# Cross-attention with image tokens: one wait split in the output product, one K load cut in two, one output weight loaded a step later

## The chip, the cores and the metric

The kernel runs on one core of a Trainium2 chip. The metric is the device time of one execution in microseconds (us). Before the change three runs gave 409.63, 410.31 and 410.38 us; their median is 410.31 us.

## The reference

The layer is a cross-attention of 4096 query rows (2 batches of 2048) with 640 features and 20 heads of 32. Each batch has 77 context tokens: 69 of text and 8 for the image (4 dummy tokens, 4 for boxes), each group with weights and a softmax of its own.

```python
q = split_heads(x @ w_q)                       # 20 heads of 32
k = split_heads(text @ w_k);    v = split_heads(text @ w_v)        # 69 tokens, depth 1024
out_text = softmax(q @ k.T / sqrt(32)) @ v
k_ip = split_heads(ip @ w_k_ip); v_ip = split_heads(ip @ w_v_ip)   # 8 tokens
out_ip = softmax(q @ k_ip.T / sqrt(32) + mask_ip(bbox)) @ v_ip     # mask 0 or -10000
return (out_text + out_ip) @ w_out + b_out + x
```

Everything is float32. The kernel makes the products with w_q and w_out from high and low parts of their factors.

## The kernel before

**Units.** The work is 40 units, numbered c. A unit is one block of 128 of the 640 features (4 heads), g = c mod 5, for one tile of 512 query rows. Five units in a row, g = 0 to 4, are a group: one tile of rows of one batch. The features lie on the partitions, the rows on the free axis.

**Split products.** A factor such as x is stored as x_hi, its rounding to the matmul's reduced float format, and x_lo, the rest. A product over depth 640 is then 15 matmuls (`product`, L631 to L636): for each of five blocks kt of 128 of the depth, hi by hi, hi by lo and lo by hi, so that matmul n belongs to block n // 3. `make_q` makes the queries of a unit so, `make_out` its block of the output. The output of unit c needs the attention output of all five units of its group as its five depth blocks: matmuls 0 to 11 read the blocks of units c to c+3 of the group's first unit c, matmuls 12 to 14 the block of unit c+4.

**A unit's way.** TensorE makes the scores (`make_scores`, L666); VectorE takes the maximum and subtracts it (L499 to L516); ScalarE takes the exponential (L393); VectorE sums and inverts (L523 to L528); GpSimd multiplies by the inverse (L355, L357); VectorE transposes 32 by 32 blocks (L535); SyncE issues eight DMAs of the result (L257) and ScalarE four (L401); TensorE makes the attention output o (`make_o`, L680); ScalarE copies it to o_hi (L436); VectorE makes o_lo = o - o_hi (L541); later TensorE makes the output product, and VectorE adds bias and residual (`finish`, L553).

**Order of the work.** Every engine has an order of its own, written out by hand: a prologue, 40 steps, an epilogue. In step c of the middle part TensorE does `make_scores(c+1)`, `make_o(c-2)`, `make_q(c+2)`, `make_out(c-6)`. VectorE does the maximum and shift of unit c+1, `o_low(c-2)`, the transpose of c, the sums of c+1, `finish(c-6)`. ScalarE does `o_high(c-2)`, the exponential of c+1, the copy of q of c+2, its four DMA issues for c, and then the high parts of what was loaded in this step. GpSimd does the multiplication of c and then the low parts of what was loaded in step c-1. Each engine works its list strictly in order, so a wait holds everything behind it on that engine. `make_out(c)` with g = 0 waits until `o_low` of unit c+4 is done, which VectorE does in the same step; the last group's outputs are made by another function (`make_last`) in the epilogue.

**Loads.** x tiles and the five blocks of w_q and of w_out pass through five slots of a tile named stage, in the order of the list JOBS; SyncE loads a slot (L239), ScalarE makes the high part (L380 for x, L383 for weights), the low part follows on GpSimd (L339, L343). x of the next group is loaded in steps with g = 0 (three tiles) and g = 1 (two). WO_JOBS says in which steps the blocks of w_out are loaded: blocks 0 and 1 in step 4, 2 in step 6, 3 in step 7, 4 in step 8. The first output product is that of step 6.

**Prologue.** SyncE issues, in this order, w_q block 0, five tiles of x, the context, the first image K weights (wki), the first K weights (wk, 512 KB, L244), the grid, the boxes, the identity (eye), w_q 1, wk 1, wki 1, w_q 2; the next load waits for a K block to be finished. TensorE warms up, makes q of unit 0, then `k_image(0)` (L716), `k_text(0)` (L710, eight depth blocks), `k_fold(0)` (L734) and the scores of unit 0, then `k_text(1)` and more. In steps 0 to 5 it also makes the rest of K and V; for V block g the order is `v_image(g)` (L716), four matmuls of a q, `v_fold(g)` (L749), which waits until ScalarE has copied the image part (`copy_v_part`, L412), the rest of q with `v_turn(g)` (L754) in it.

Of the kernel before, what the change touches and what calls it, by code (L numbers as in the profile page):

```python
# [11 lines left out]
P = 128  # L12
# [13 lines left out]
KD = D // P  # L26
KC = C // P
# [12 lines left out]
K_SLOTS, V_SLOTS, AHEAD_K = 2, 3, 2  # L40
# [1 line left out]
V_OLD = {3: 0, 4: 2}  # L42
V_OLD_STEP = {V_OLD[g] + 1: g for g in V_OLD}
X_JOBS = {0: (0, 1, 2), 1: (3, 4)}
WO_JOBS = {4: (0, 1), 6: (2,), 7: (3,), 8: (4,)}
BEHIND_OUT = KD + 1


def xattn_kernel(nc, x, ctx, bbox, grid, eye, w_q, w_k, w_v, w_k_ip, w_v_ip, w_out, b_out, out):
# [5 lines left out]
    def sb(name, shape, dt=F32):  # L55

        at[name] = top[0]
        n = 4
        for s in shape[1:]:
            n *= s  # L60
        top[0] += -(-n // 32) * 32
        assert top[0] <= nc.sbuf_usable_end, (name, top[0], nc.sbuf_usable_end)
        return nc.alloc_sbuf_tensor_at(name, shape, dt, offset=at[name])

    def over(name, owner, shape, offset=0):

        return nc.alloc_sbuf_tensor_at(name, shape, F32, offset=at[owner] + offset)

    def sem(name):
        return es.enter_context(nc.semaphore(name))  # L70

    with es:
# [7 lines left out]
        k = sb("k", [P, BATCH, KD, TOKENS])  # L80
# [24 lines left out]
        half = KD * W * 4  # L105
        x0_raw = over("x0_raw", "o_lo", [P, KD, W])
        wk_raw = over("wk_raw", "o_hi", [P, K_SLOTS, KC, P], half)
# [29 lines left out]
        bias_loaded = sem("bias_loaded")  # L137
        ctx_loaded = sem("ctx_loaded")
        wk_loaded = [sem(f"wk_loaded{s}") for s in range(K_SLOTS)]
        wki_loaded = [sem(f"wki_loaded{s}") for s in range(K_SLOTS)]  # L140
        wv_loaded = [sem(f"wv_loaded{s}") for s in range(V_SLOTS)]
        wvi_loaded = [sem(f"wvi_loaded{s}") for s in range(V_SLOTS)]
# [27 lines left out]
        o_lo_done = sem("o_lo_done")  # L170
# [6 lines left out]
        def place(c):  # L177

            return (c // KD) % BATCH, c // (BATCH * KD), c % KD
# [23 lines left out]
        def out_bank(c):  # L203

            return Q_BANK if c == UNITS - BEHIND_OUT - 1 else OUT_BANK
# [10 lines left out]
        def step_jobs(c):  # L216

            if c in WO_JOBS:
                jobs = [("w_out", g) for g in WO_JOBS[c]]
            else:  # L220
# [10 lines left out]
        def _(sp):  # L231
            def load(job):

                what, n = job
                src, width = {"w_q": (w_q, D), "w_out": (w_out, D), "x": (x, W)}[what]
                number = NUMBER[job]
                if number >= KD:
                    sp.wait_ge(stage_lo, number - KD + 1)
                sp.dma_start(stage[:, number % KD, 0:width], src[n]).then_inc(stage_loaded[number % KD], 16)  # L239

            def load_k(g, dst, src, loaded):
                if g >= K_SLOTS:
                    sp.wait_ge(kt_made, g - K_SLOTS + 1)
                sp.dma_start(dst[:, g % K_SLOTS, :, :], src[g]).then_inc(loaded[g % K_SLOTS], 16)  # L244

            def load_v(g, dst, src, loaded):
                if g in V_OLD:
                    sp.wait_ge(vt_made, V_OLD[g] + 1)
                sp.dma_start(dst[:, V_SLOT[g], :, :], src[g]).then_inc(loaded[V_SLOT[g]], 16)
# [24 lines left out]
            def prologue():  # L274
                load(("w_q", 0))
                for kt in range(KD):
                    sp.dma_start(x0_raw[:, kt, :], x[kt]).then_inc(x0_loaded[kt], 16)  # L277
                sp.dma_start(ctx_sb[:, :, :], ctx).then_inc(ctx_loaded, 16)
                load_k(0, wki_raw, w_k_ip, wki_loaded)
                load_k(0, wk_raw, w_k, wk_loaded)  # L280
                sp.dma_start(grid_sb[:, :], grid).then_inc(grid_loaded, 16)
                sp.dma_start(box[:, :, :, :], bbox).then_inc(grid_loaded, 16)
                sp.dma_start(eye_sb[:, :], eye).then_inc(eye_loaded, 16)
                load(("w_q", 1))
                load_k(1, wk_raw, w_k, wk_loaded)
                load_k(1, wki_raw, w_k_ip, wki_loaded)
                load(("w_q", 2))
                load_k(2, wk_raw, w_k, wk_loaded)
                load_k(2, wki_raw, w_k_ip, wki_loaded)
                load(("w_q", 3))  # L290
                load_v(0, wv_raw, w_v, wv_loaded)
                load_v(0, wvi_raw, w_v_ip, wvi_loaded)
                load(("w_q", 4))
                load_v(1, wv_raw, w_v, wv_loaded)
                load_v(1, wvi_raw, w_v_ip, wvi_loaded)
                load_k(3, wk_raw, w_k, wk_loaded)
                load_k(3, wki_raw, w_k_ip, wki_loaded)
# [20 lines left out]
            def epilogue():  # L318
# [6 lines left out]
                for k in range(2):  # L325
                    sp.wait_ge(stored[k], 16 * (UNITS // 2))

            turns(prologue, step, epilogue)

        @block.gpsimd  # L330
# [297 lines left out]
        def _(pe):  # L628
            whole = range(3 * KD)

            def product(bank, w_hi, w_lo, m_hi, m_lo, b, g, n):  # L631

                kt = n // 3
                w, m = ((w_hi, m_hi), (w_hi, m_lo), (w_lo, m_hi))[n % 3]
                return nc.tensor.matmul(ps[:, bank, :], w[:, g, P * kt:P * kt + P], m[:, b, kt, :],  # L635
                                        start=(n == 0), stop=(n == 3 * KD - 1))  # L636
# [48 lines left out]
            def make_out(c):  # L685
                b, t, g = place(c)
                if g == 0:
                    pe.wait_ge(o_lo_done, c + KD)
                if c < KD:
                    pe.wait_ge(stage_lo, NUMBER[("w_out", g)] + 1)  # L690
                if out_bank(c) == Q_BANK:
                    pe.wait_ge(q_copied, UNITS)
                elif c >= 1:
                    pe.wait_ge(finished, c if out_bank(c - 1) == OUT_BANK else c - 1)
                for n in whole:
                    last = product(out_bank(c), wo_hi, wo_lo, o_hi, o_lo, b, g, n)
                last.then_inc(out_made, 1)

# [19 lines left out]
                last.then_inc(made, 1)  # L718

            def k_text(g, kts=range(KC)):  # L720
                pe.wait_ge(wk_loaded[g % K_SLOTS], 16 * (g // K_SLOTS + 1))
                if g >= 2:
                    pe.wait_ge(k_copied, g if g > 2 else 1)
                text_part(k_places[g], wk_raw[:, g % K_SLOTS, :, :], kts)
# [32 lines left out]
            def prologue():  # L757
                pe.wait_ge(zeros_set, 1)
                for n in range(WARM):
                    nc.tensor.matmul(ps[:, WARM_BANK, 0:P], q[:, 0, 0:P], q[:, 0, 0:P], start=True, stop=True)  # L760
                make_q(0, whole)
                pe.wait_ge(ctx_loaded, 16)
                k_image(0)
                k_text(0)
                k_fold(0)
                make_scores(0)
                k_text(1)
                make_q(1, whole[0:6])
                k_image(1)
                make_q(1, whole[6:15])  # L770
                k_text(2)
                k_fold(1)
                k_image(2)
# [103 lines left out]
```

## Time and profile before

| | |
|---|---|
| median of three runs | 410.31 us |
| profiled execution, its time | 409.03 us |
| profiled execution, its span | 407.2 us |
| TensorE busy with matmuls | 397.4 us, 98% |
| VectorE busy | 337.1 us, 83% |
| GpSimd busy | 155.9 us, 38% |
| ScalarE busy | 129.3 us, 32% |
| granted TensorE clock, mean | 1.000 |
| HBM read, written | 35.53 MB, 10.49 MB |

The span runs from the first to the last instruction; the time has the work around it as well, here 1.8 us. Matmuls are pipelined: a 128x512 matmul lasts some 0.39 us in the profile but the next one starts 0.23 us after it, so that the time of TensorE is read from the starts and not from the busy share. An idle time is shown in brackets with what ended it.

### The profile page before, as it was taken

The page shows a single profiled execution, that of the slowest core. Times are in us where ns is not written, and L with a number is a line of the kernel's source. Part 1 is how long each engine was busy: PE and PEld are TensorE (multiplying, and loading weights), DVE is VectorE, ACT ScalarE, POOL GpSimd, SP SyncE. Part 2 cuts the span into 40 slices and gives each one's busy share as a digit, 9 for nine tenths or more (in the row PEclk, how much of TensorE's full clock was granted, in tenths as well). Part 3 has the DMA queues.
Part 4 walks back from the last instruction along what each step waited for, and adds up shares of the span by engine and source line. Part 5 has one row for each costly group of instructions (what it writes and reads, how often), then busy time and mean ns, then how long its engine had stood idle before and what let it go on. Part 6 is the DMA issues. An engine that isn't in the chain of part 4 may idle for free.

```text
span 407.2 us, 10795 instructions
## 1 busy us (share of the span) xinstructions
PE 397.4 (98%) x4452; PEld 290.7 (71%) x4452; DVE 337.1 (83%) x458; ACT 129.3 (32%) x196; POOL 155.9 (38%) x128
## 2 busy tenths in 40 slices
PE   7899999899999999999999999999999999999996
PEld 6688878567777776777777767777776767776764
DVE  4559779899999988999989988999988898989523
ACT  5236343463333322432323322333223322232100
POOL 0336622686326433363226533462226532222200
PEclk9999999999999999999999999999999999999999
DMA  7999746675567455764566454764466453544655
GB/s 276 360 381 341 203 133 184 181 198 164 172 172 200 140 138 144 201 166 129 148 180 213 131 137 134 206 167 125 139 192 208 137 134 119 143 136 118 168 154 196
DMA packets 42849, 72.96 MB, mean 179 GB/s; under 512 B 10544, under 2 KB 10672, under 8 KB 42800
## 3 DMA queue, kind: packets, MB, share of 16 engines
q1 hardware_dynamic: 37680, 67.02, 54.3%
q10 hardware_dynamic: 5120, 5.25, 5.9%
q8 instruction: 35, 0.57, 0.6%
q14 instruction: 14, 0.11, 0.1%
HBM read 35.53 MB, written 10.49 MB: 113 GB/s over the span
## 4 chain that ended last, share of the span: by engine, by line
PE 81%; DVE 5%; DMA 5%; SPq 4%; issue 2%; ACT 2%; ACTq 1%; DVEq 0%
PE ps L635 59%; PE ps L666 8%; PE ps L680 8%; PE ps L710 3%; SPq L257 2%; DMA out_tiles<-res 2%; DMA wk_raw<-in_w_k 2%; DVE text_max L499 1%; DVE prob L505 1%; ACT prob L393 1%; ACTq L401 1%; PE ps L716 1%; DMA res<-in_x 1%; SPq L277 1%; SPq L268 1%
## 5 line engine op out<-in xcount | busy, mean ns | idle before, releaser
L355 POOL TENSOR_TENSOR prob<-prob,rden 128x1104 f32<-128x1104 f32 x40 | 82.3, 2056 | 205.5 <-DVE rden L528 205.5
L635 PE MATMUL ps<-x_hi,wq_hi 128*128 128x512 f32 x200 | 83.2, 416 | 1.6 <-DVE x_lo L597 1.6
L635 PE MATMUL ps<-o_hi,wo_hi 128*128 128x512 f32 x200 | 80.2, 401 | 0.4 <-DVE o_lo L541 0.4
L635 PE MATMUL ps<-o_hi,wo_lo 128*128 128x512 f32 x200 | 78.9, 395 | 0.0
L635 PE MATMUL ps<-o_lo,wo_hi 128*128 128x512 f32 x200 | 78.9, 395 | 0.0
L635 PE MATMUL ps<-x_lo,wq_hi 128*128 128x512 f32 x200 | 78.7, 394 | 0.0
L635 PE MATMUL ps<-x_hi,wq_lo 128*128 128x512 f32 x200 | 78.1, 391 | 0.0
L393 ACT ACTIVATE prob<-prob 128x1232 f32<-128x1232 f32 x40 | 50.0, 1250 | 68.9 <-DVE prob L516 68.9
L535 DVE STREAM_TRANSPOSE prob_t<-prob 128x1536 f32<-128x1536 f32 x40 | 70.6, 1766 | 0.2 <-POOL prob L357 0.2
L499 DVE TENSOR_REDUCE text_max<-ps 128x16 f32<-128x1104 f32 x40 | 52.1, 1303 | 19.5 <-PE ps L666 19.4
L635 PEld LDWEIGHTS ps<-x_hi,wq_hi 128*128 128x128 f32 x200 | 37.5, 187 | 36.8 <-issue 28.0
L523 DVE TENSOR_REDUCE den<-prob 128x16 f32<-128x1104 f32 x40 | 50.5, 1263 | 7.1 <-ACT prob L393 7.1
L436 ACT ACTIVATE o_hi<-ps 128x512 fp32r<-128x512 f32 x40 | 23.7, 593 | 102.8 <-PE ps L680 98.9
L505 DVE TENSOR_TENSOR prob<-ps,text_max 128x1104 f32<-128x1104 f32 x40 | 51.9, 1299 | 0.0
L635 PEld LDWEIGHTS ps<-o_hi,wo_hi 128*128 128x128 f32 x200 | 37.5, 188 | 14.8 <-issue 3.4
L553 DVE SCALAR_TENSOR_TENSOR res<-ps,bias,res 128x512 f32<-128x512 f32 x37 | 27.4, 741 | 22.3 <-PE ps L635 11.2
L339 POOL TENSOR_TENSOR x_lo<-stage,x_hi 128x512 fp32r<-128x512 f32 x35 | 44.8, 1305 | 2.7 <-ACT x_hi L380 2.7
L635 PEld LDWEIGHTS ps<-o_hi,wo_lo 128*128 128x128 f32 x200 | 37.5, 188 | 9.3
L635 PEld LDWEIGHTS ps<-o_lo,wo_hi 128*128 128x128 f32 x200 | 37.5, 188 | 8.5
L635 PEld LDWEIGHTS ps<-x_hi,wq_lo 128*128 128x128 f32 x200 | 37.6, 188 | 8.2
L666 PEld LDWEIGHTS ps<-k,q 32*64 32x64 f32 x2560 | 32.6, 130 | 14.4 <-issue 12.6
L680 PE MATMUL ps<-prob_k,v 77*32 77x512 f32 x320 | 42.6, 605 | 0.3 <-DMA prob_k<-prob_t 0.3
(58 smaller groups left out, 350.1 us busy)
## 6 DMA issues: line engine op xcount, KB each, us to landing
prob_k<-prob_t SPq DMA_DIRECT2D x320, 64.0 KB
stage<-in_x SPq DMA_DIRECT2D x38, 256.0 KB, 3.1
res<-in_x SPq DMA_DIRECT2D x37, 256.0 KB
out_tiles<-res SPq DMA_DIRECT2D x37, 256.0 KB, 2.3
prob_k<-prob_t ACTq DMA_DIRECT2D x160, 32.0 KB
wki_raw<-in_w_k_ip SPq DMA_DIRECT2D x5, 512.0 KB, 7.4
wk_raw<-in_w_k SPq DMA_DIRECT2D x5, 512.0 KB, 7.3
wv_raw<-in_w_v SPq DMA_DIRECT2D x5, 512.0 KB, 7.3
```

Of the source, the lines that this page charges most:

```text
L339: nc.gpsimd.tensor_tensor(x_lo[:, b, kt, :], slot[:, 0:W], x_hi[:, b, kt, :].bitcast(F32), ALU.subtract).then_inc(stage_lo, 1)
L355: nc.gpsimd.tensor_tensor(e[:, :, 0:TEXT], e[:, :, 0:TEXT], rden[:, par, 0, :].unsqueeze(2).to_broadcast([P, QT * HG, TEXT]), ALU.mult)
L393: nc.scalar.activation(prob[:, c % 2, :, 0:TOKENS], prob[:, c % 2, :, 0:TOKENS], ACT.Exp).then_inc(exp_done, 1)
L436: nc.scalar.activation(o_hi[:, b, g, :], ps[:, O_BANK, :], ACT.Copy).then_inc(o_hi_done, 1)
L499: nc.vector.tensor_reduce(text_max[:, par, :, :], s[:, :, :, 0:TEXT], AX_X, ALU.max).then_inc(text_max_done, 1)
L505: nc.vector.tensor_tensor(e[:, :, :, 0:TEXT], s[:, :, :, 0:TEXT], text_max[:, par, :, :].unsqueeze(3).to_broadcast([P, QT, HG, TEXT]), ALU ...
L523: nc.vector.tensor_reduce(den[:, par, 0, :], e[:, :, 0:TEXT], AX_X, ALU.add)
L535: nc.vector.transpose(prob_t[:, c % 2, :, :, :].rearrange("p k n r -> p n k r"), prob[:, c % 2, :, :].rearrange("p n (k r) -> p n k r", r= ...
L553: nc.vector.scalar_tensor_tensor(out=tile, in0=ps[:, bank, :], scalar=bias[:, c % KD:c % KD + 1], in1=tile, op0=ALU.add, op1=ALU.add).then ...
L635: return nc.tensor.matmul(ps[:, bank, :], w[:, g, P * kt:P * kt + P], m[:, b, kt, :], start=(n == 0), stop=(n == 3 * KD - 1))
L666: last = nc.tensor.matmul(ps[at:at + P // 2, j, TOKENS * n:TOKENS * n + TOKENS], q[rows, c % 2, P * n + at:P * n + at + P // 2], k[rows, b ...
L680: last = nc.tensor.matmul(ps[DH * j:DH * j + DH, O_BANK, :], v[0:TOKENS, b, P * g + DH * j:P * g + DH * j + DH], p_k[:, :, :, j, :], start ...
```

## The change

Three things are changed. First, `make_out` of a group's first unit waits at its start for four `o_low` of the group's five and for the fifth before its matmul 12, the thirteenth. Second, the first K weights are loaded by two DMAs of four depth blocks each, with a semaphore each, and `k_text(0)` is called in two halves that wait for one semaphore each; the counts of the other K loads are shifted to match. Third, block 1 of w_out is loaded in step 5, behind the three x tiles of that step, where it was loaded in step 4; its high part moves on ScalarE from step 4 to step 5, its low part on GpSimd from step 5 to step 6.

```diff
-WO_JOBS = {4: (0, 1), 6: (2,), 7: (3,), 8: (4,)}
+WO_JOBS = {4: (0,), 5: (1,), 6: (2,), 7: (3,), 8: (4,)}
...
+        wk0_loaded = [sem(f"wk0_loaded{h}") for h in range(2)]
...
-                load_k(0, wk_raw, w_k, wk_loaded)
+                for half in range(2):
+                    kts = slice(KC // 2 * half, KC // 2 * half + KC // 2)
+                    sp.dma_start(wk_raw[:, 0, kts, :], w_k[0].rearrange("p (k n) -> p k n", n=P)[:, kts, :]).then_inc(wk0_loaded[half], 16)
...
                 if g == 0:
-                    pe.wait_ge(o_lo_done, c + KD)
+                    pe.wait_ge(o_lo_done, c + KD - 1)
...
                 for n in whole:
+                    if g == 0 and n == 3 * KD - 3:
+                        pe.wait_ge(o_lo_done, c + KD)
                     last = product(out_bank(c), wo_hi, wo_lo, o_hi, o_lo, b, g, n)
...
             def k_text(g, kts=range(KC)):
-                pe.wait_ge(wk_loaded[g % K_SLOTS], 16 * (g // K_SLOTS + 1))
+                if g == 0:
+                    pe.wait_ge(wk0_loaded[kts[0] * 2 // KC], 16)
+                else:
+                    pe.wait_ge(wk_loaded[g % K_SLOTS], 16 * ((g + 1) // K_SLOTS))
...
-                k_text(0)
+                k_text(0, range(0, KC // 2))
+                k_text(0, range(KC // 2, KC))
```

## Rows read from the trace of the kernel before

**Rows 1.** Busy time by stretch: length, busy (instructions) by engine, clock, DMA share, GB/s.

```profile
100.00:363.00 263.00, 262.94 (x2959) 188.69 (x2958) 237.46 (x320) 81.25 (x114) 105.12 (x85) 1.00 0.56 158
```

**Rows 2.** Waits, whole span: us in total, times, longest.

```profile
PEld ps L635 <- DVE o_lo L541: 3.1, 7, 0.8
```

**Rows 3.** Timeline of PE at three of the seven first output products: start, us.

```profile
83.96 0.39 PE L635 MATMUL ps<-x_hi,wq_lo 128*128 128x512 f32 x1
...
85.05 0.39 PE L635 MATMUL ps<-o_lo,wo_hi 128*128 128x512 f32 x1
...
129.70 0.39 PE L635 MATMUL ps<-x_hi,wq_lo 128*128 128x512 f32 x1
...
130.44 0.39 PE L635 MATMUL ps<-o_lo,wo_hi 128*128 128x512 f32 x1
...
356.82 0.39 PE L635 MATMUL ps<-x_hi,wq_lo 128*128 128x512 f32 x1
...
357.29 0.39 PE L635 MATMUL ps<-o_lo,wo_hi 128*128 128x512 f32 x1
```

**Rows 4.** Timeline of DVE and PE in the first q product, which waits five times.

```profile
7.14 2.66 DVE L597 TENSOR_TENSOR x_lo<-x_raw,x_hi 128x512 fp32r<-128x512 f32 x4 [1.18 <-ACT x_hi L442]
...
9.86 0.39 PE L635 MATMUL ps<-x_hi,wq_lo 128*128 128x512 f32 x1
10.09 0.39 PE L635 MATMUL ps<-x_hi,wq_hi 128*128 128x512 f32 x1
```

**Rows 5.** Timeline of PE, first K block and start of the second.

```profile
11.57 0.64 PE L716 MATMUL ps<-wki_raw,ctx_sb 128*32 128x128 f32 x16 [0.63 <-DMA wki_raw<-in_w_k_ip]
12.84 2.15 PE L710 MATMUL ps<-ctx_sb,wk_raw 128*128 128x138 f32 x16 [0.62 <-DMA wk_raw<-in_w_k]
...
16.46 2.15 PE L710 MATMUL ps<-ctx_sb,wk_raw 128*128 128x138 f32 x16
```

**Rows 6.** Timeline of SP's queue, the five x tiles.

```profile
1.18 2.32 SPq L277 DMA_DIRECT2D x_raw<-in_x  x5
```

**Rows 7.** DMA issues of x tiles four and five: KB, us to landing.

```profile
x_raw<-in_x SPq DMA_DIRECT2D x1, 256.0 KB, 5.2
...
x_raw<-in_x SPq DMA_DIRECT2D x1, 256.0 KB, 5.3
```

**Rows 8.** DMA issues at 6.05 (eye) and 7.28 (second K block): us to landing.

```profile
eye_sb<-in_eye SPq DMA_DIRECT2D x1, 72.0 KB, 7.3
...
wk_raw<-in_w_k SPq DMA_DIRECT2D x1, 512.0 KB, 7.9
```

**Rows 9.** Timeline of ACT and PE in step 5, at v_fold(4).

```profile
73.21 1.37 ACT L383 ACTIVATE wo_hi<-stage 128x640 fp32r<-128x640 f32 x2 [3.56 <-issue]
74.48 0.26 ACT L412 ACTIVATE img_part<-ps 128x128 f32<-128x128 f32 x1
...
73.94 0.40 PE L635 MATMUL ps<-x_hi,wq_hi 128*128 128x512 f32 x1
74.79 0.40 PE L749 MATMUL ps<-eye_sb,img_part 128*128 128x16 f32 x2 [0.46 <-ACT img_part L412]
```

**Rows 10.** Timeline of DVE, ACT and POOL in step 6 and at its end.

```profile
83.97 0.68 DVE L541 TENSOR_TENSOR o_lo<-ps,o_hi 128x512 fp32r<-128x512 f32 x1
...
88.50 0.75 DVE L553 SCALAR_TENSOR_TENSOR res<-ps,bias,res 128x512 f32<-128x512 f32 x1 [0.40 <-PE ps L635]
...
81.36 1.68 ACT L380 ACTIVATE x_hi<-stage 128x512 fp32r<-128x512 f32 x3 [2.66 <-issue]
82.94 0.58 ACT L436 ACTIVATE o_hi<-ps 128x512 fp32r<-128x512 f32 x1
...
82.60 3.86 POOL L339 TENSOR_TENSOR x_lo<-stage,x_hi 128x512 fp32r<-128x512 f32 x3
```

**Rows 11.** Landing times of all loads into the stage slots.

```profile
DMA to landing us min/median/max: 2.2/3.1/8.9
```

**Rows 12.** Timeline of DVE at the scores of the last unit.

```profile
370.94 1.31 DVE L499 TENSOR_REDUCE text_max<-ps 128x16 f32<-128x1104 f32 x1 [0.45 <-PE ps L666]
```

## The prediction

> **What bounds the kernel now.** Read the page first: TensorE is busy 98% of the span, VectorE 83%, the rest far less, the clock is at full throughout. The table of stretches sharpens this: between 100 and 363 us, 29 steps, TensorE has 262.94 of 263.00 us and VectorE 237.46 [rows 1]. VectorE so has 25.5 us to spare, 0.88 us in each step. The reader is to see that in this stretch only time on TensorE counts, and that a gain there is followed by VectorE as long as it is under 0.88 us a step. But busy is no proof of full pace, as ends of matmuls are modelled. So I read the waits next: the weight load ahead of the output product waits for o_lo seven times, 3.1 us in all [rows 2], which the matmul row hides. Last the timeline, start by start, at each of these seven places and wherever TensorE's row shows a bracket. Those in the part that the diff touches: 0.62 us for the first K weights [rows 5] and 0.46 us for the copied image part of V block 4 [rows 9].
>
> **The late wait in make_out.** What one wait costs is the distance from the last q matmul to the second output matmul. Where nothing is late it is 357.29 - 356.82 = 0.47 us, two normal steps [rows 3]. In the first output product it is 85.05 - 83.96 = 1.09, so 0.62 us are lost; at 129.70 it is 0.74, so 0.27. The four like it, at 175, 220, 266 and 311 us, read 0.71, 0.73, 0.73 and 0.77: 0.24, 0.26, 0.26 and 0.30. The seventh, at 356.82, loses nothing. Sum: 0.62 + 0.27 + 0.24 + 0.26 + 0.26 + 0.30 + 0 = 1.95 us. (The 3.1 us of rows 2 count the idle weight load, which in a full stream also rests between loads, so the starts are the better measure.)
>
> After the change the product starts behind the q product, and the wait comes twelve matmuls later, at 0.233 us each 2.8 us. o_lo was late by at most 0.7 us. So it is there 2 us ahead, and what is late next is nothing on this path. Twelve of the fifteen matmuls are issued before the wait; queued behind it are the last three and then the next scores, which VectorE waits for, but only if the wait bites.
>
> Does a satisfied wait amid a product cost anything? The first q product has such waits, at its matmuls 3, 6, 9 and 12. x_lo of the fifth tile is done by 7.14 + 2.66 = 9.80 us; the thirteenth matmul starts at 10.09, 0.23 us behind the one before it [rows 4]. That is the normal distance: the price is nil, here with no more than 0.3 us in hand. I take 0 for seven added waits and 1.95 us gained. For the bounds: were each satisfied wait to cost a quarter of a matmul step, 0.06 us, it would be 0.4 us in seven.
>
> Does the gain stay? VectorE waits for TensorE both at finish (0.40 us, at 88.50) [rows 10] and at the next maximum (0.45 us, as at 370.94) [rows 12]; each group of five steps gets 0.27 us shorter against five times 0.88 us to spare. At 370.94 VectorE still waits for the last scores, so that what follows, the transpose, its DMAs and the chain of stores and residual loads which ends the kernel, starts earlier by as much as TensorE does. This chain of some 30 us is of waits between DMAs, none bound to a fixed time; I price its change at 0, with 0.5 us of chance either way.
>
> **First K weights in halves.** k_image(0) starts at 11.57, as its weights land; its sixteen short matmuls hold until 12.21. k_text(0) starts at 12.84, as wk has landed [rows 5]. The two 512 KB transfers land 1.27 us apart, so half of one takes some 0.64 us: the first half lands at about 12.1, before TensorE is free, the second at 12.8. Four of the eight depth blocks take about 1.0 us (all eight take 2.15 us, less a modelled tail of some 0.2), so the second half is called at 13.2 and has 0.4 us in hand. Gain: 12.84 - 12.24 = 0.60 us.
>
> Smaller transfers might be slower, with rows of 2 KB where they were 4 KB. The x tiles have such rows: tile five is issued 0.47 us after tile four [rows 6] and takes 5.3 where that took 5.2 us [rows 7], so they land 0.57 us apart, 256 KB each; at the pace of the K weights 256 KB take 0.64. No loss, then. One more issue costs SyncE 0.47 us [rows 6] for everything behind it in the prologue; these transfers take 7.3 to 8.3 us to land where the same kind takes 3.1 later [rows 8, 11], so they stand in line and an issue 0.5 us later changes nothing. Were it to, by the whole 0.47: the identity lands at 6.05 + 7.3 + 0.47 = 13.8, before the fold that wants it (about 14.2); wk 1 lands at 7.28 + 7.9 = 15.2, or 15.7, and is wanted at 16.46 - 0.60 = 15.86. Behind that the loads wait for the fold of block 0 and so move with it. I keep 0.60, with 0.2 to 0.65 as bounds.
>
> The Trainium skill speaks against this edit: "DMA: Bandwidth & Descriptors", in its section on the anatomy of one DMA, gives each DMA a constant part of about 2.0 us beside its bytes, and its section on bandwidth wants transfers of 1 MiB and up. If the two halves paid that one after the other, by its figures the second half would land some 2 us later, an estimate from that page. Rows 7 show the opposite for transfers in line, 0.57 us apart, and so the rule, which measures one alone, gets a small chance below.
>
> **w_out block 1 a step later.** In step 5 ScalarE makes two high parts, from 73.21 to 74.58, and only then copies the image part of V block 4, at 74.48; TensorE stops after the matmul of 73.94 and starts v_fold(4) at 74.79 [rows 9]. Unheld it would start at 73.94 + 0.23 = 74.17: 0.62 us lost. With one high part fewer (half of the 1.37, some 0.65 us) the copy starts at 73.83 and is done at 74.09 + a little: v_fold(4) starts on time. Gain 0.62 us, at worst 0.5. SyncE's issue of that load (0.46 us) moves behind the x loads of step 5, ahead of a residual that is wanted twelve us later.
>
> What it adds in step 6: on ScalarE, in front of the copy to o_hi of unit 4 at 82.94 [rows 10], 0.65 us. The copy then ends near 83.59 + 0.58 = 84.2 and o_lo of unit 4 starts at 84.2 for 83.97 and ends at 84.9. Before the change this would have been on TensorE's path; now the thirteenth matmul waits for it, and that one is due at 83.96 + 0.23 - 0.62 + 2.80 = 86.4. It has 1.5 us in hand. VectorE itself runs 0.25 us later and has the 0.40 and the 0.45 us. On GpSimd the low part (about 1.3 x 640/512 = 1.6 us) runs behind the three x tiles, 82.60 + 3.86 + 1.6 = 88.1, as the sums of unit 7 are ready (88.50 - 0.40): no delay, at worst 0.1. The block itself is wanted by the second output product at 93 us.
>
> **Sum.** 1.95 + 0.60 + 0.62 = 3.17 us. The profiled execution took 409.03 us (span 407.2), which gives 405.9 (span 404.0). It was 1.28 us faster than the median of the three runs, so against that median: 410.31 - 3.2 = 407.1 us.
>
> **The rivals.**
> - One small term fails: a load behind the split, or the stop at v_fold, stays. The 0.4 us in hand for the second half and the exact fit at 74.17 speak for it. Gain 3.2 - 0.6 = 2.6 us: 407.7.
> - Transfers pay their fixed part each (the page's rule, told with rows): the shortest landing of a stage load is 2.2 us [rows 11]. If the second half took that behind the first, 12.1 + 2.2 = 14.3, k_text(0) would end at 15.3 for 14.8: 0.5 us lost instead of 0.6 gained. Gain 2.1: 408.2. The tiles of x speak against it.
> - The tail absorbs it: the last 30 us hang on SyncE's stores and residual loads, and if these start no earlier the end stays. 410.3. Against it: VectorE's 0.45 us wait at 370.94.
> - Slower: the moved load. It stands behind three x loads, issued at about 76.4 us by SyncE's timeline, and ScalarE, strictly in order, wants it at 83.0. Should it land later, o_lo of unit 4 and TensorE at the thirteenth matmul are late by as much beyond 1.5 us. With the longest landing of any stage load, 8.9 us [rows 11], it comes at 85.3 and costs 85.3 - 83.0 - 1.5 = 0.8 us: still faster. It turns the sign only from a landing 83.0 + 1.5 + 3.2 + 0.8 = 88.5 on, 12 us after its issue, as four times the median of 3.1 us; then 411.2.
>
> **How the numbers follow.** Forecast 0.70, one term failing 0.14, fixed parts 0.05, tail 0.06, slower 0.03; 0.02 remain for the unthought. About 0.2%, 0.8 us, is what a measurement of this kernel can tell from no change. So faster 0.90, same 0.07, slower 0.03. The runs before span 0.75 us; with the bounds of the terms (gain 2.4 to 3.8) and that, the range is 406.0 to 408.7 us, which holds the first two rivals as well.
>
> **What would show it.** In the trace after: no wait of PE or PEld for o_lo, and 0.23 us between all starts at the six places; k_text(0) at 12.2 to 12.3 without a stop at its fifth block; v_fold(4) 0.23 us behind its matmul; o_lo of unit 4 about 0.2 us later against the scores of its step; the clock still 1.00. I am wrong if a wait of 0.3 us or more turns up at a thirteenth matmul, if K loads behind the split hold TensorE, if the scores or make_o begin to wait in the middle part, or if the last 30 us grow.

## The result, and the profile after

The changed kernel took 406.56 us (median of six runs, 405.89 to 407.92) beside 409.51 us for the kernel before on the same chip (six runs, 409.27 to 410.38). The medians are 2.95 us apart; the ratio on record is 0.9917, with an interval of 0.9900 to 0.9933: 3.4 us faster, 2.7 to 4.1. The forecast was 407.1 us and a gain of 3.2, counted from a median of three runs of 410.31 us; the six runs' median is 0.8 us lower. One run of all those told below was slow (414.56 us, the kernel with the moved load alone), and the ratios leave it out. The profiled execution took 406.34 us with a span of 404.5, so 2.7 us less than the profiled execution before.

The page of the changed kernel, its span and its busy time by engine:

```profile
span 404.5 us, 10796 instructions
...
PE 396.8 (98%) x4452; PEld 292.2 (72%) x4452; DVE 337.2 (83%) x458; ACT 129.5 (32%) x196; POOL 155.8 (39%) x128
```

Its stretch of 100 to 363 us, same columns as [rows 1]:

```profile
100.00:363.00 263.00, 263.00 (x2964) 190.24 (x2963) 238.33 (x322) 82.78 (x114) 103.76 (x84) 1.00 0.57 160
```

The busy share hardly moved (TensorE 262.94 to 263.00 us of 263.00); five more matmuls went through the same 263 us. That is all a busy row can show of a gain of 1.2 us here. The list of waits of the changed kernel has no row in which TensorE or its weight load waits for o_lo, where [rows 2] had 3.1 us. The starts show where the gain is. The timeline of TensorE after, at the places of [rows 5], [rows 9] and [rows 3], and at the last attention output (L638 is the former L635, L715 L710, L721 L716, L757 L749, L669 L666):

```profile
11.33 0.64 PE L721 MATMUL ps<-wki_raw,ctx_sb 128*32 128x128 f32 x16 [0.60 <-DMA wki_raw<-in_w_k_ip]
11.90 2.15 PE L715 MATMUL ps<-ctx_sb,wk_raw 128*128 128x138 f32 x16
...
73.31 0.40 PE L638 MATMUL ps<-x_hi,wq_hi 128*128 128x512 f32 x1
73.55 0.39 PE L757 MATMUL ps<-eye_sb,img_part 128*128 128x16 f32 x2
...
77.51 0.95 PE L669 MATMUL ps<-k,q 32*64 32x77 f32 x64 [0.69 <-ACT q L392]
...
82.69 0.39 PE L638 MATMUL ps<-x_hi,wq_lo 128*128 128x512 f32 x1
83.15 0.39 PE L638 MATMUL ps<-o_lo,wo_hi 128*128 128x512 f32 x1
...
85.49 0.40 PE L638 MATMUL ps<-o_hi,wo_lo 128*128 128x512 f32 x1
85.72 0.39 PE L638 MATMUL ps<-o_hi,wo_hi 128*128 128x512 f32 x1
...
127.72 0.39 PE L638 MATMUL ps<-x_hi,wq_lo 128*128 128x512 f32 x1
128.18 0.39 PE L638 MATMUL ps<-o_lo,wo_hi 128*128 128x512 f32 x1
...
388.28 1.07 PE L683 MATMUL ps<-prob_k,v 77*32 77x512 f32 x8 [0.45 <-DMA prob_k<-prob_t]
```

The reader is to see three things. k_text(0) starts 0.57 us behind k_image(0), where it was 1.27. v_fold(4) starts 0.24 us behind its matmul, where it was 0.85. And from the last q matmul to the second output matmul it is 0.46 us at the first output product and at the next, where it was 1.09 and 0.74; the thirteenth matmul, at 85.72, stands 0.23 us behind the twelfth.

Laid over the trace before, start against start, TensorE stands so:

| place (time before, us) | TensorE ahead, us |
|---|---|
| k_image(0) (11.57) | 0.24 |
| k_text(0) (12.84) | 0.94 |
| first matmul of V block 1 (44.4) | 0.80 |
| behind v_fold(1) (49.6) | 0.62 |
| v_fold(4) (74.8) | 1.24 |
| in the first output product | 1.88 |
| in the five later groups' (130 to 312) | 2.26, 2.54, 2.84, 3.00, 3.24 |
| at 357 | 3.19 |
| last attention output (391.2) | 2.94 |
| span | 2.7 |

The start at 0.24 is no part of the change: the image weights landed earlier in this execution. Each of these five groups brings 0.16 to 0.38 us, the last of the seven nothing, as the row of 357.29 in [rows 3] has it. From 357 us on 0.5 us are given back.

Behind the late wait stood VectorE's subtraction ahead of o_low (L516), and behind that GpSimd. VectorE and GpSimd of the kernel before at the second group:

```profile
128.86 0.59 DVE L516 TENSOR_TENSOR prob<-prob,img_max 128x128 f32<-128x128 f32 x1
129.37 0.68 DVE L541 TENSOR_TENSOR o_lo<-ps,o_hi 128x512 fp32r<-128x512 f32 x1
...
128.01 1.28 POOL L339 TENSOR_TENSOR x_lo<-stage,x_hi 128x512 fp32r<-128x512 f32 x1
```

L516 takes 0.29 us where nothing stretches it. Here it takes 0.59 and ends 0.15 us behind GpSimd's low part of x, and o_lo follows at once. It is stretched by 0.70 us in the first group and by 0.25 to 0.30 in the next five; the waits cost 0.62 and 0.24 to 0.30. In the last group no tile of x is left to load, L516 takes 0.29 us and the wait costs nothing. This is read from the trace; no run here takes GpSimd's low parts away.

### The profile page after: what moved, and what is told of

Same layout as the page of the kernel before. It is cut to its first block, busy times and chain, and to the rows that moved or that the text cites. A ratio compares the mean times of both kernels' runs of the same rounds, so it can differ in the third digit from the quotient of the medians.

```text
span 404.5 us, 10796 instructions
## 1 busy us (share of the span) xinstructions
PE 396.8 (98%) x4452; PEld 292.2 (72%) x4452; DVE 337.2 (83%) x458; ACT 129.5 (32%) x196; POOL 155.8 (39%) x128
## 4 chain that ended last, share of the span: by engine, by line
PE 85%; DMA 5%; SPq 4%; DVE 3%; ACT 1%; issue 1%; DVEq 0%
PE ps L638 62%; PE ps L683 9%; PE ps L669 9%; PE ps L715 4%; SPq L258 2%; DMA out_tiles<-res 2%; DMA wki_raw<-in_w_k_ip 2%; PE ps L721 1%; DMA res<-in_x 1%; DVE text_max L502 1%; DVE prob L508 1%; ACT prob L396 1%; SPq L278 1%; SPq L269 1%; ACT q L392 0%
## 5 line engine op out<-in xcount | busy, mean ns | idle before, releaser
L638 PE MATMUL ps<-x_hi,wq_hi 128*128 128x512 f32 x200 | 83.3, 417 | 0.6 <-DVE x_lo L600 0.6
L638 PE MATMUL ps<-o_hi,wo_hi 128*128 128x512 f32 x200 | 79.6, 398 | 0.0
L638 PE MATMUL ps<-o_hi,wo_lo 128*128 128x512 f32 x200 | 79.0, 395 | 0.0
L638 PE MATMUL ps<-o_lo,wo_hi 128*128 128x512 f32 x200 | 78.9, 395 | 0.0
L638 PE MATMUL ps<-x_lo,wq_hi 128*128 128x512 f32 x200 | 78.7, 393 | 0.0
L638 PE MATMUL ps<-x_hi,wq_lo 128*128 128x512 f32 x200 | 78.2, 391 | 0.0
L638 PEld LDWEIGHTS ps<-x_hi,wq_hi 128*128 128x128 f32 x200 | 37.6, 188 | 35.8 <-issue 28.2
L638 PEld LDWEIGHTS ps<-o_hi,wo_hi 128*128 128x128 f32 x200 | 37.5, 188 | 12.0 <-issue 3.4
L638 PEld LDWEIGHTS ps<-o_hi,wo_lo 128*128 128x128 f32 x200 | 37.5, 188 | 9.2
L638 PEld LDWEIGHTS ps<-o_lo,wo_hi 128*128 128x128 f32 x200 | 37.5, 188 | 8.8
L638 PEld LDWEIGHTS ps<-x_hi,wq_lo 128*128 128x128 f32 x200 | 37.6, 188 | 8.3
L669 PEld LDWEIGHTS ps<-k,q 32*64 32x64 f32 x2560 | 32.6, 130 | 14.5 <-issue 12.6
```

Source lines behind the costliest of these rows:

```text
L669: last = nc.tensor.matmul(ps[at:at + P // 2, j, TOKENS * n:TOKENS * n + TOKENS], q[rows, c % 2, P * n + at:P * n + at + P // 2], k[rows, b ...
```

## The experiments

### The split wait alone

```diff
-                    pe.wait_ge(o_lo_done, c + KD)
+                    pe.wait_ge(o_lo_done, c + KD - 1)
...
+                    if g == 0 and n == 3 * KD - 3:
+                        pe.wait_ge(o_lo_done, c + KD)
```

> The kernel before with only the split wait in make_out. Theory (TensorE bounds; each late wait costs what its start distance shows): gain 1.95 us, ratio 0.995, and in the trace 0.23 us between all starts at the six places; the stop at v_fold(4), 0.62 us, and the one for the first K weights, 0.6 us, stay. Rival (VectorE or the tail takes the time back): under 1 us.

Measured: 407.71 us, ratio 0.9944 (0.9924 to 0.9965), span 406.2. Up to the first output product TensorE moves between 0.5 us ahead of the trace before and 0.3 behind, and is 0.03 us ahead just before it; at 357 us it is 2.07 us ahead. All seven distances are 0.46 or 0.47. By 389 us 0.55 us are lost again at the last attention output.

The stop at v_fold(4) that I had expected to stay was not there: the unmoved load did not cost here what it had. ScalarE, TensorE, VectorE and GpSimd of this kernel around V block 4, to be read against [rows 9]:

```profile
72.38 1.37 ACT L383 ACTIVATE wo_hi<-stage 128x640 fp32r<-128x640 f32 x2 [2.67 <-issue]
73.65 0.26 ACT L412 ACTIVATE img_part<-ps 128x128 f32<-128x128 f32 x1
...
74.24 0.39 PE L635 MATMUL ps<-x_hi,wq_hi 128*128 128x512 f32 x1
74.47 0.29 PE L751 MATMUL ps<-eye_sb,img_part 128*128 128x16 f32 x2
78.75 0.95 PE L666 MATMUL ps<-k,q 32*64 32x77 f32 x64 [1.13 <-ACT q L389]
...
75.31 1.63 DVE L516 TENSOR_TENSOR prob<-prob,img_max 128x128 f32<-128x128 f32 x1
...
73.69 3.10 POOL L343 TENSOR_TENSOR wo_lo<-stage,wo_hi 128x640 fp32r<-128x640 f32 x2
```

Both high parts are still there (1.37 us), but ScalarE's four DMA issues ahead of them took 2.84 us, where the trace before had 3.98, so the copy was in time. The 0.4 us went elsewhere: VectorE's L516 lasted 1.63 us, until 0.15 us behind the end of GpSimd's two low parts, and the next scores waited 1.13 us for their q instead of 0.69.

### The halves alone

```diff
+                for half in range(2):
+                    kts = slice(KC // 2 * half, KC // 2 * half + KC // 2)
+                    sp.dma_start(wk_raw[:, 0, kts, :], ...).then_inc(wk0_loaded[half], 16)
```

> The kernel before with only the first K weights in two transfers. Theory: TensorE 0.6 to 0.7 us earlier from k_text(0) on. The trace of the changed kernel shows 0.93 us there, of which 0.24 were an earlier landing of the image weights, and only 0.62 left at 50 us; so two rivals for the end: the 0.3 us given back between 43 and 48 us belongs to this edit (ScalarE's copies and the loads do not move with TensorE): gain 0.4 us; or it belongs to the loads' chance: gain 0.6 to 0.7. The rival that transfers pay a fixed part each would make it slower.

Measured: 408.66 us, ratio 0.9972 (0.9958 to 0.9987), span 405.8. TensorE of this kernel at the first K block and at the first output product:

```profile
10.71 0.64 PE L719 MATMUL ps<-wki_raw,ctx_sb 128*32 128x128 f32 x16 [0.92 <-DMA wki_raw<-in_w_k_ip]
11.29 2.15 PE L713 MATMUL ps<-ctx_sb,wk_raw 128*128 128x138 f32 x16
...
81.78 0.39 PE L638 MATMUL ps<-x_hi,wq_lo 128*128 128x512 f32 x1
...
82.89 0.40 PE L638 MATMUL ps<-o_lo,wo_hi 128*128 128x512 f32 x1
```

k_text(0) follows k_image(0) after 0.58 us and runs as one row of sixteen matmuls. The unsplit wait of this kernel cost 1.11, 0.66, 0.65, 0.46, 0.51, 0.70 and 0.53 us of distance, less 0.47 each: 1.33 us, where the trace before lost 1.95. What a late wait costs differs between executions; that it costs nothing once split does not. The ratio alone says 0.5 to 1.7 us faster. Of the two rivals, the trace bears out the second: TensorE is 1.55 us ahead of the trace before at k_text(0), 0.86 of it by earlier image weights, and 1.54 at 50 us, so nothing is given back. From the first output product to 357 us it nevertheless falls back by 0.23 us, though its late waits there cost less than before. The time goes to the scores: from the first of a unit's 64 score matmuls to the first matmul of make_o it is 0.88 us at the shortest, but the thirty units between 85 and 352 us take 27.98 us here and 27.17 in the trace before. The rows name no engine and no DMA that it waits for there; what stretches them stays open.

### The moved load alone

```diff
-WO_JOBS = {4: (0, 1), 6: (2,), 7: (3,), 8: (4,)}
+WO_JOBS = {4: (0,), 5: (1,), 6: (2,), 7: (3,), 8: (4,)}
```

> The kernel before with only w_out block 1 loaded a step later. Theory by this case's rows: v_fold(4) starts 0.62 us earlier, but the first output product still waits at its first matmul for o_lo of unit 4, which ScalarE's moved high part makes 0.2 us later: the gain is lost there, the end is 0 to 0.3 us later than before, ratio 1.000 to 1.001. Rival (the terms add up whatever stands beside them): 0.6 us faster, ratio 0.9985.

Measured: 409.83 us (median of all twelve runs), ratio 0.9986 (0.9962 to 1.001), span 408.6: no difference that can be told, so that the trace has to decide between my theory and its rival. This execution had lost 0.80 us against the trace before by 72 us, part of it to the fourth K weights. v_fold(4), unheld, brought that down to 0.18; behind the first output product it was 0.14. I had expected the unsplit wait there to take the gain back. It did not: from the last q matmul on the stop was 0.10 us longer, no more. ScalarE, VectorE and TensorE of this kernel in step 6, for [rows 10] and [rows 3]:

```profile
82.84 0.74 ACT L383 ACTIVATE wo_hi<-stage 128x640 fp32r<-128x640 f32 x1 [0.32 <-DMA stage<-in_w_out]
83.49 0.58 ACT L436 ACTIVATE o_hi<-ps 128x512 fp32r<-128x512 f32 x1
...
83.13 1.00 DVE L516 TENSOR_TENSOR prob<-prob,img_max 128x128 f32<-128x128 f32 x1
84.10 0.69 DVE L541 TENSOR_TENSOR o_lo<-ps,o_hi 128x512 fp32r<-128x512 f32 x1
...
84.00 0.39 PE L635 MATMUL ps<-x_hi,wq_lo 128*128 128x512 f32 x1
...
85.19 0.39 PE L635 MATMUL ps<-o_lo,wo_hi 128*128 128x512 f32 x1
```

The distance is 85.19 - 84.00 = 1.19 us, where [rows 3] have 1.09. The high part does push o_hi back, to 84.07. But VectorE reaches o_lo only at 84.10, after an L516 of 1.00 us, so the delay on ScalarE is covered. So the cover is an L516 of 1.00 us, and it took 0.99 in the trace before. It does not always cover: in both traces of the reordered kernel below o_hi is done last, 0.53 and 0.62 us behind L519, and o_lo starts with it.

### The split wait with the moved load

The two edits above together.

> The split wait and the moved load, first K weights in one transfer. Theory: 1.95 + 0.62 = 2.57 us faster, ratio 0.9937, so the moved load is worth 0.6 us beside the split wait and nothing without it; the stop for the first K weights stays at 0.6 us. Rival (parts independent): the same here, and only the run with the moved load alone tells them apart.

Measured: 407.76 us, ratio 0.9942 (0.9922 to 0.9963), span 406.0. TensorE is 0.82 us ahead at v_fold(4), which starts 0.24 us behind its matmul, 1.50 in the first output product, 1.87 in the second group's and 2.30 at 357 us. From v_fold(4) on that is 1.48 us, where the theory had 1.95; all seven distances are 0.46, and the thirty units' scores take 0.49 us more than in the trace before. The times do not show the moved load: 0.9942 with it beside 0.9944 without.

### The changed kernel again

No edit.

> The changed kernel again, as the measure for the three that follow on the same chip: 3.2 us faster than before, ratio 0.992. What was given back between 43 and 48 us in its first trace (0.3 us) comes again if it is the kernel's, not if it was chance.

Measured: 407.22 us (twelve runs, 405.48 to 409.24), ratio 0.994 (0.9916 to 0.9964), span 407.2. The profiled execution is one of its bad ones, and so of use. TensorE of this execution where it lost most:

```profile
28.93 0.39 PE L638 MATMUL ps<-x_hi,wq_lo 128*128 128x512 f32 x1
30.70 0.97 PE L715 MATMUL ps<-ctx_sb,wk_raw 128*128 128x138 f32 x6 [1.39 <-DMA wk_raw<-in_w_k]
```

TensorE lost 1.57 us waiting for the fourth K weights, which took 6.6 us from issue to landing. In the first profile of the changed kernel the same load took 4.6 us and nobody waited; in the kernel before it was 4.7. Between 41 and 50 us it gives back 0.6 us, so what the first trace gave back there came again; but the split wait alone, without halves, gives back 0.54 there, and halves alone and the third execution of the changed kernel nothing. Its issue in this execution, KB and us to landing:

```profile
wk_raw<-in_w_k SPq DMA_DIRECT2D x1, 512.0 KB, 6.6
```

Over all fourteen traces this wait cost 1.57, 1.18, 0.45, 0.37 and 0.20 us in five, whose loads took 6.6, 6.2, 5.5, 5.4 and 5.3 us, and nothing in nine, whose loads took 4.4 to 5.1. So TensorE wants these weights some 5.0 us behind their issue, with halves and without. One of the five (0.45, the moved load alone) has no halves. Four of ten with halves against one of four without is too few to say whether halves make a long landing likelier; that stays open.

### Many satisfied waits

```diff
                     if g == 0 and n == 3 * KD - 3:
                         pe.wait_ge(o_lo_done, c + KD)
+                    elif n:
+                        pe.wait_ge(o_lo_done, c - g + (KD - 1 if g == 0 else KD))
```

> The changed kernel with a wait that is already satisfied ahead of each of the matmuls 1 to 14 of all 35 output products of make_out, 483 more waits. Theory (a satisfied wait costs TensorE nothing): the time of the changed kernel within 0.3 us and 0.23 us between starts. Rival (a satisfied wait costs a quarter of a matmul step, 0.06 us): 29 us slower. A price of 0.01 us each would be 5 us.

Measured: 406.4 us, ratio 0.9923 (0.99 to 0.9946), span 403.9, beside 407.22 us and 0.994 for the changed kernel on the same chip. 483 more waits in 35 output products cost nothing that shows. TensorE of this kernel in the second group, a wait ahead of the last three matmuls:

```profile
127.75 0.40 PE L638 MATMUL ps<-o_hi,wo_hi 128*128 128x512 f32 x1
127.98 0.39 PE L638 MATMUL ps<-o_lo,wo_hi 128*128 128x512 f32 x1
128.21 0.40 PE L638 MATMUL ps<-o_hi,wo_lo 128*128 128x512 f32 x1
128.45 0.40 PE L638 MATMUL ps<-o_hi,wo_hi 128*128 128x512 f32 x1
```

The steps are 0.23 and 0.24 us, as without waits.

### The second wait at the fourth matmul

```diff
-                    if g == 0 and n == 3 * KD - 3:
+                    if g == 0 and n == 3:
```

> The changed kernel with the wait for the fifth low part ahead of matmul 3 instead of 12, 0.7 us behind the product's start. Theory (late by 0.2 to 0.3 us in five groups, by 0.8 in the first): the five are covered, the first loses 0.1 to 0.2 us; time as the changed kernel within 0.3 us. Rival (the place is what counts, since VectorE falls behind TensorE once the wait no longer holds it): waits show up in all groups and 1 us or more is lost.

Measured: 407.66 us, ratio 0.9949 (0.9927 to 0.9971), span 404.0: the changed kernel's time beside it (407.22) to within the intervals. TensorE and VectorE of this kernel at the first output product:

```profile
82.34 0.40 PE L638 MATMUL ps<-o_hi,wo_hi 128*128 128x512 f32 x1
...
83.04 0.41 PE L638 MATMUL ps<-o_hi,wo_hi 128*128 128x512 f32 x1
...
82.21 0.69 DVE L544 TENSOR_TENSOR o_lo<-ps,o_hi 128x512 fp32r<-128x512 f32 x1
```

o_lo is done at 82.90, the fourth matmul starts at 83.04, on the grid of 0.23 us to within 0.02. So three matmuls in hand are enough in this execution, by 0.14 us, where I had expected 0.1 to 0.2 us lost. It is close: the weight load ahead of this matmul did wait 0.2 us for o_lo, which the matmul row hides. In the six other groups nothing waits. Of the twelve matmuls that the change puts ahead of the wait nine are reserve.

### The changed kernel without the moved load

```diff
-WO_JOBS = {4: (0,), 5: (1,), 6: (2,), 7: (3,), 8: (4,)}
+WO_JOBS = {4: (0, 1), 6: (2,), 7: (3,), 8: (4,)}
```

> The split wait and the halves, w_out block 1 loaded in step 4 as before. In three traces so far without the moved load v_fold(4) was held only where ScalarE's four DMA issues ahead of it took 3.98 us (0.62 us lost), not where they took 2.84 and 3.35 us; where they took 2.84 us, GpSimd's two low parts in a row held VectorE's L516 (1.63 us for 0.29) and the copy of q came 0.44 us later. Theory: the moved load is worth what chance decides, 0 to 0.6 us, so this is 0 to 0.6 us slower than the changed kernel, ratio to before 0.992 to 0.994. Rival (a fixed 0.62 us): v_fold(4) is held here again by 0.5 to 0.7 us whatever the issues take.

Measured: 406.97 us, ratio 0.9935 (0.9911 to 0.9959), span 405.6, beside 405.85 us and 0.9916 for the changed kernel on the same chip (its run is told below); the intervals overlap. v_fold(4) starts 0.59 us behind its matmul, 0.35 us late:

```profile
73.63 0.40 PE L638 MATMUL ps<-x_hi,wq_hi 128*128 128x512 f32 x1
74.22 0.40 PE L757 MATMUL ps<-eye_sb,img_part 128*128 128x16 f32 x2 [0.19 <-ACT img_part L415]
```

### Three blocks of w_out in step 4

```diff
-WO_JOBS = {4: (0,), 5: (1,), 6: (2,), 7: (3,), 8: (4,)}
+WO_JOBS = {4: (0, 1, 2), 7: (3,), 8: (4,)}
```

> The changed kernel with blocks 0, 1 and 2 of w_out all loaded in step 4: two more high parts, 0.65 us each, on ScalarE ahead of the copy that v_fold(4) waits for, and two more low parts on GpSimd. Theory (ScalarE's order is the cause of the stop): v_fold(4) held by 0.2 to 1.4 us, according to its DMA issues (2.8 to 4.0 us), and L516 lengthened beyond 1 us: 0.7 to 1.5 us slower than the changed kernel. Rival (the stop was a late load or something else of that trace): no more than 0.2 us at v_fold(4).

Measured: 407.74 us, ratio 0.9946 (0.9926 to 0.9966), span 405.2. ScalarE and TensorE of this kernel at v_fold(4):

```profile
71.28 1.99 ACT L386 ACTIVATE wo_hi<-stage 128x640 fp32r<-128x640 f32 x3 [2.72 <-issue]
...
72.85 0.40 PE L638 MATMUL ps<-x_hi,wq_hi 128*128 128x512 f32 x1
73.48 0.40 PE L757 MATMUL ps<-eye_sb,img_part 128*128 128x16 f32 x2 [0.24 <-ACT img_part L415]
```

Short issues (3.13 us) and a third high part give 0.39 us of stop. With the traces above, of v_fold(4):

| high parts ahead of the copy | issues, us | v_fold(4) behind its matmul, us |
|---|---|---|
| 2 (before) | 3.98 | 0.85 |
| 2 (without the moved load) | 3.67 | 0.59 |
| 2 (halves alone) | 3.35 | 0.24 |
| 2 (split wait alone) | 2.84 | 0.23 |
| 3 | 3.13 | 0.63 |
| 1 (nine traces) | 2.94 to 3.96 | 0.23 to 0.24 |

So the stop comes from the sum of the issues and the high parts: 3.98 + 1.37 = 5.35 held it 0.62 us, 3.67 + 1.37 = 5.04 held it 0.35, 3.13 + 1.99 = 5.12 held it 0.39, and 4.72 or less held nothing. One high part fewer keeps it under that even with issues of 3.96 us. The price that I expected of this edit besides, a long L516, did not come: it started 0.24 us before the running low part ended and lasted 0.39 us. The medians are 1.9 us apart (407.74 beside 405.85, ratios 0.9946 and 0.9916); 0.39 us of it is explained. The profiled execution took 406.96, one of the shortest of its ten, and does not show the rest.

### The attention output ahead of the scores in step 6

```diff
+                    if c == KD + 1:
+                        make_o(c - 2)
+                        make_scores(c + AHEAD_S)
+                    else:
                     make_scores(c + AHEAD_S)
                     make_o(c - 2)
```

> The changed kernel with make_o(4) ahead of make_scores(7) in step 6. TensorE stops there for 0.69 us (0.85 us beyond the normal distance) while ScalarE copies the q it needs next. Theory: make_o(4) fills that stop, as its DMAs land by about 76.5 us: 0.8 us faster than the changed kernel, 4.0 faster than before, ratio 0.990. Rival (the scores come 0.15 us later for VectorE, whose order is full from 71 us on, or make_o waits for its DMAs): 0 to 0.3 us.

Measured: 405.85 us (nine runs), ratio 0.9918 (0.9894 to 0.9943), span 404.0. The scores of unit 7 waited 0.69 us for their q in the changed kernel; here the attention output fills that. TensorE of this kernel:

```profile
76.20 0.40 PE L638 MATMUL ps<-x_hi,wq_lo 128*128 128x512 f32 x1
76.53 1.06 PE L683 MATMUL ps<-prob_k,v 77*32 77x512 f32 x8
78.56 0.50 PE L638 MATMUL ps<-x_hi,wq_hi 128*128 128x512 f32 x1
```

From the last q matmul of the step before to the first of this one it is 2.36 us; in the changed kernel it was 79.39 - 76.42 = 2.97. At 90 us TensorE is 0.80 us further on than in the first trace of the changed kernel, 0.22 of it from before this step, and in the last 35 us it loses 0.87 of its lead on the trace before. It was run once more, beside the changed kernel:

> The version with make_o(4) ahead of make_scores(7) again, beside the changed kernel. Its first trace had TensorE 0.63 us further at 90 us than the changed kernel, 0.8 expected, and lost 0.8 in the last 30 us to a wait for DMAs. Theory (the loss at the end was chance): 0.6 us faster than the changed kernel. Rival (the gain turns into a longer wait of the last make_o): the same time.

Measured: 407.01 us (twelve runs), ratio 0.9935 (0.9912 to 0.9959), span 405.8; the step 0.76 us shorter (2.21 us), but 1.18 us lost at the fourth K weights and 0.84 us idle at the last attention output.

> The changed kernel a third time, beside the three others on this chip. Theory: 2.5 to 3.4 us faster than before; no stop at v_fold(4), k_text(0) 0.58 us behind the start of k_image(0), no wait for o_lo. Open: whether TensorE waits for the fourth K weights at about 29 us as in one of its two traces (1.39 us) or not, as in the other.

The changed kernel beside it: 405.85 us (six runs), ratio 0.9916 (0.9889 to 0.9942), span 404.0. So the reordered kernel, at 0.9918 and 0.9935, is not shown to beat the changed one, at 0.994 and 0.9916 beside it. Its gain of 0.61 and 0.76 us shows in its step of the two traces, and is smaller than what the loads at 30 us and the last attention output take in one execution and not in the next.

## Why the prediction was right

The forecast of 407.1 us came 0.5 us too high. Counted from the median of all six runs before, 409.51 us, the same gain of 3.2 would have given 406.3, 0.2 below what was measured. Two of the signs that the prediction named for being wrong did turn up, both small: the last 30 us grew by 0.5 us in the pair, and K loads behind the split held TensorE, not in the pair but in four of the ten traces with halves.

**The late wait: right in mechanism and size.** Predicted 1.95 us. In the pair of profiles TensorE goes from 1.24 us ahead at v_fold(4) to 3.19 ahead at 357 us, which is 1.95; alone the edit took it from 0.03 to 2.07. A satisfied wait was priced at nil from one row with 0.3 us in hand; 483 of them confirm it. The claim of 2 us in hand at the thirteenth matmul holds: with the wait at the fourth, 2.1 us earlier, it was still just in time. All eleven traces with the split show 0.46 to 0.47 us at all seven places. What was too exact is the 1.95 as a property of the kernel: executions with the unsplit wait lost 1.95, 1.46 and 1.33. And that 1.95 came out of the pair to the hundredth is luck: laid over the trace before in the same way, the nine traces with the split wait and the old order of step 6 gained 1.48 to 2.58 us from v_fold(4) to 357 us, for the units' scores there took 26.79 to 27.75 us in sum, and 27.17 in the trace before.

**The halves: right in the pair, with a cover that was overrated.** Predicted 0.60, measured 1.27 - 0.57 = 0.70: k_image(0) holds TensorE for 0.57 us, not 0.64. In all ten traces with halves the start distance is 0.57 to 0.60 and no second half was late. The estimate from the Trainium skill, "DMA: Bandwidth & Descriptors", section on the anatomy of one DMA, of a second half some 2 us later did not come true for these transfers, which stand in line: TensorE asks for the second half 1.05 us behind the first matmul and never waited. (The Trainium skill has its 2.0 us in that section from transfers that GpSimd issues; these are SyncE's.) The step that failed is "Behind that the loads wait for the fold of block 0 and so move with it". They do, and TensorE wants the fourth K weights as long behind their issue as before; but their time on the way varies: 4.4 to 6.6 us for the same 512 KB, against a reserve of about 0.4 us at k_text(3) in the trace before. I had looked for delays by the extra issue, and not asked how wide the landing times spread. Whether the halves make a long landing likelier, the runs leave open.

**The moved load: the gain shows in traces, is not fixed, and no time shows it.** Predicted 0.62 us, measured 0.62 in the pair, on the same issue time (3.98 and 3.96 us); that the trace before was the one with the longest issues of all is luck. Over the other traces with two high parts the stop was 0, 0 and 0.35 us, by how long ScalarE's four issues take. The times with and without the moved load lie within each other's intervals in all three pairs (0.9986 and no change, 0.9942 and 0.9944, 0.9916 and 0.9935). The added cost on o_lo of unit 4, predicted as 0.2 us, did not come by the way predicted: in the pair o_lo starts 0.28 us later against the scores of its step (5.50 and 5.22 us behind them), but VectorE's own L516 was the later one, not o_hi. ScalarE, VectorE and GpSimd of the changed kernel, for [rows 10]:

```profile
81.61 0.72 ACT L386 ACTIVATE wo_hi<-stage 128x640 fp32r<-128x640 f32 x1
82.24 0.58 ACT L439 ACTIVATE o_hi<-ps 128x512 fp32r<-128x512 f32 x1
...
82.09 1.00 DVE L519 TENSOR_TENSOR prob<-prob,img_max 128x128 f32<-128x128 f32 x1
83.01 0.68 DVE L544 TENSOR_TENSOR o_lo<-ps,o_hi 128x512 fp32r<-128x512 f32 x1
...
81.64 3.87 POOL L342 TENSOR_TENSOR x_lo<-stage,x_hi 128x512 fp32r<-128x512 f32 x3
85.46 1.57 POOL L346 TENSOR_TENSOR wo_lo<-stage,wo_hi 128x640 fp32r<-128x640 f32 x1
87.21 2.06 POOL L358 TENSOR_TENSOR prob<-prob,rden 128x1104 f32<-128x1104 f32 x1 [0.18 <-DVE rden L531]
```

o_hi is done at 82.82, o_lo starts at 83.01 as L519 ends and is done at 83.69, 2.0 us ahead of the thirteenth matmul at 85.72. GpSimd is through with the low part of 1.57 us at 87.03, before the sums are ready: the 1.6 and the "no delay" of the forecast.

**The sum.** 1.95 + 0.62 + 0.70 = 3.27 us, and 0.24 for the image weights that landed earlier, less 0.32 at 30 to 50 us (part of it at v_fold(1), whose copy came late), makes 3.19 at 357 us. The tail was priced at 0 with 0.5 either way and took 0.5: 2.7 in the span. The rival that the tail absorbs all of it fell. But the last attention output hangs on DMAs and cost 0.01 to 0.58 us beyond the trace before in every one of the thirteen, never less. That this is the tail eating part of the gain is not shown: the moved load alone, with no gain left at 357 us, lost 0.27 there, and the wait at the fourth matmul, with 3.2, lost 0.01. The trace before simply has the shortest stop there of all fourteen. The slower case, a late w_out block 1, did not show: ScalarE waited at most 0.32 us for it, and the thirteenth matmul never waited.

The three parts alone gave ratios of 0.9944, 0.9972 and 0.9986, which makes 0.990 if they add up; all together gave 0.9917, 0.994 and 0.9916. Within their intervals of some 0.2% either way they add. Clear of no change alone are the split wait and the halves.

## What to carry to other kernels

A product of several depth blocks should wait for each block where it first reads it; the wait costs nothing once it is satisfied, and a busy row hides what it costs while it is late, so measure the distance of starts. When a time is taken from one profile, ask for the spread of the transfers and issues that it leans on: terms of a few tenths of a microsecond behind a DMA are there in one execution and gone in the next; and when the sum comes out to the hundredth, lay other executions over it too; only the wait put at its first read stayed free in all eleven traces. To rank versions 0.6 us apart at 400 us, lay the traces start by start over one another; medians of the changed kernel in three measurements differed by 1.4 us.

## What was not expected of the hardware

- VectorE's subtraction of 128x128 elements (L516, L519 after) takes 0.29 us at the least. In 202 of its 560 executions in the fourteen traces it takes 0.46 to 1.63 us, and every one of these ends 0.15 us behind the end of one of GpSimd's low parts (`x_lo`, `wq_lo`, `wo_lo`) that overlaps it. What it costs is what is left of GpSimd's instruction, and in step 6 this set when o_lo could start.
- The 64 score matmuls of a unit take 0.88 us up to the first matmul of make_o, and up to 1.29 us in single steps; the rows name nothing that it waits for (the idle time in between is put down to issue), and over thirty units executions differ by 1.2 us.
- Four DMA issues of ScalarE took from 2.84 to 3.98 us at one and the same place of the program in different executions.
- One 512 KB load at one place took between 4.4 and 6.6 us from issue to landing.
- Two loads of 256 KB, cut from one of 512 KB, are not slower in a row than the whole: TensorE reads through both without a stop.
